# One step of delay for the cross attention's addition and an earlier first feed-forward batch in a decoder's head loop

## The reference

```python
x = x + mixer(layernorm(x))              # u @ W_b_rank @ W_b_state, butterfly of 5 levels, @ W_c_rank @ W_c_model, + D_vec * u
x = x + cross(layernorm(x), ctx, mask)   # softmax(x ctx^T / 16) ctx, no projections
x = x + ffn(layernorm(x))                # three bit-linear layers: activations rounded to 127 levels of their row's
                                         # maximum, weights to -1, 0, 1 of their mean magnitude; silu(gate) * value
...
```

## Time and profile before

| | |
|---|---|
| median of 3 runs | 1234.73 us (1233.15 to 1235.99) |
| the profiled execution's own time | 1230.95 us |
| its span | 1229.2 us |
| mean granted clock | 0.947 of full |
| DVE, ACT, POOL busy | 71%, 53%, 27% of the span |
| head, up to the first feed-forward product on DVE | 0 to 105.11 us |

### The profile page before, as it was taken

One profiled execution on the slowest core, in us unless ns is written; L12 is line 12 of the kernel. 1 busy time (PEld: TensorE's weight loads), 2 busy tenths in 40 slices (PEclk: granted clock), 3 DMA queues, 4 the chain that ended last, 5 costly groups with the idle time before them and its releaser, 6 DMA issues.

```text
span 1229.2 us, 21690 instructions
## 1 busy us (share of the span) xinstructions
PE 1058.1 (86%) x6401; PEld 729.3 (59%) x6409; DVE 874.5 (71%) x2446; ACT 654.7 (53%) x1989; POOL 333.1 (27%) x528
## 2 busy tenths in 40 slices
PE   5767887899899958899999999999998998998395
PEld 3553444666666634565667666656666665675285
DVE  4566675777887767868957778678678677765275
ACT  2757775565555615556545565565555445642262
POOL 2224231211111222313213223133132132111456
PEclk9877999999999978899999999999999999999598
...
DMA packets 38876, 49.59 MB, mean 40 GB/s; under 512 B 5110, under 2 KB 29564, under 8 KB 38528
## 3 DMA queue, kind: packets, MB, share of 16 engines
...
...
## 4 chain that ended last, share of the span: by engine, by line
PE 38%; DVE 11%; issue 6%; POOL 3%; ACT 3%; DVEq 0%; DMA 0%; ACTq 0%; POOLq 0%
PE PS L1784 35%; POOL out_dram L1376 3%; DVE arena L815 2%; DVE arena L791 1%; PE PS L2161 1%; DVE arena L827 1%; PE PS L2138 1%; ACT arena L1626 1%; POOL tokens_dram L1352 1%; DVE arena L801 1%; DVE arena L797 1%; ACT arena L1635 1%; DVE small L849 0%; DVE early L724 0%; DVE early L719 0%
## 5 line engine op out<-in xcount | busy, mean ns | idle before, releaser
L1784 PE MATMUL PS<-early,arena 128*32 128x128 f32 (+6 forms) x920 | 123.3, 362 | 51.3 <-DVE early L681 24.3
L1784 PE MATMUL PS<-EW,arena 128*128 128x128 f32 (+4 forms) x640 | 134.4, 341 | 18.0 <-DVE small L815 10.8
L1784 PE MATMUL PS<-wq,EW 128*128 128x512 f32 x256 | 128.6, 626 | 13.1 <-DVE arena L791 12.7
L1290 POOL TENSOR_SCALAR small<-small 128x4 f32<-128x4 f32 x64 | 18.8, 294 | 429.4 <-ACT mask L1619 251.6
L1784 PEld LDWEIGHTS PS<-EW,arena 128*128 128x128 f32 x640 | 99.5, 193 | 48.9 <-issue 23.5
L1784 PEld LDWEIGHTS PS<-early,arena 128*32 128x32 f32 (+4 forms) x928 | 63.2, 122 | 105.4 <-issue 39.4
L815 DVE CUSTOM_DVE_ANT_0 arena<-PS,kmask 128x128 f32<-128x128 f32 (+3 forms) x256 | 92.3, 389 | 42.4 <-PE PS L1784 34.0
L1635 ACT ACTIVATE arena<-arena,small 128x128 f32<-128x128 f32 (+3 forms) x256 | 119.5, 471 | 1.1 <-DVE small L820 0.9
L1626 ACT ACTIVATE arena<-PS 128x512 f32<-128x512 f32 x64 | 38.3, 598 | 153.1 <-PE PS L2138 153.1
L1784 PE MATMUL PS<-wo,early 128*128 128x256 f32 x512 | 113.3, 379 | 2.5 <-DVE sinT L868 1.7
L1784 PEld LDWEIGHTS PS<-wo,early 128*128 128x128 f32 x512 | 97.1, 190 | 16.4 <-DVE sinT L868 2.1
...
## 6 DMA issues: line engine op xcount, KB each, us to landing
...
```

What stands on the lines that cost most here:

```text
L1784: return pe.matmul(dst, lhs, rhs, start=first, stop=last)
```

## The change

- The cross attention's addition `read_out` of batch n moves from the end of step n + 1 to step n + 2, before that step's `cross_max`. Its PSUM bank is 6 instead of 3, the transposes' bank is 7 instead of 6, the sum of magnitudes' bank is 3 instead of 7.
- The mixer's normalising of batches 0 to 5 moves from ACT to DVE (`mix_apply`); ACT keeps 6 and 7. The batches have a semaphore of their own for it (`s_mxn`).
- The first feed-forward batch goes through the loop as a ninth batch of the mixer's kind: statistics and normalising into `aXN` in step 6, `prepare(0, 0)` and `rounded(0)` in step 7. `level_turn(0)`, `gate(0, 0)` and `value(0, 0)` stand on PE around the last batch's `cross_turn` and `cross_out` (`head_end`); the last `read_out` is in the first feed-forward half. On ACT `levels(0)`, `applied(1)` and the first silu stand inside step 8.
- One magnitude of each step moves ahead of ACT's exponents. The clippings move by about one step.
- Four of the seven small loads are issued by ACT; SP starts with batch 0. ACT runs one exponent on a single column right after, before it has other work.
- PE runs ten products of ones of 128 x 128 into bank 6 before its first real product.

```diff
+def stats_of(phase, b):
...
+    if phase == MIX:
+        return b if b < 2 else 2 * b - 1
+    return 2 * b + 2
...
 def added(phase, b):
...
+    if b < 0:
+        return 0
     if phase == MIX:
-        return max(1, 2 * b) if b >= 0 else 0
-    return min(2 * b + 3, 2 * B) if b >= 0 else 0
+        return b + 1 if b < 2 else 2 * b - 1
+    return 2 * b + 4 if b < B - 2 else B + 1 + b
...
 def piece(i):
...
         dve.wait_ge(s_x, n - B + 1)
-        if phase == FFN and type(b) is int and b == 0:
-            dve.wait_ge(s_rs, FFN * B)
+        if phase == FFN and type(b) is int and b == 1:
+            dve.wait_ge(s_rs, FFN * B + 1)
...
+        first = type(b) is int and b == 0
         dve.wait_ge(c_ap, b + 1)
-        dve.tensor_reduce(c_gx, XN[:, :, :], AX.X, ALU.max, apply_absolute_value=True).then_inc(c_q, 1)
+        dve.tensor_reduce(c_gx, aXN if first else XN[:, :, :], AX.X, ALU.max, apply_absolute_value=True).then_inc(c_q, 1)
         dve.wait_ge(c_q, 3 * b + 1)
...
         dve.wait_ge(c_q, 3 * b + 2)
-        dve.wait_ge(s_xn, FFN * B + b)
+        if not first:
+            dve.wait_ge(s_xn, FFN * B + b)
         dve.wait_ge(c_r, b + 1)
...
-        n = turn_of(phase, b)
-        if phase == MIX:
+        n = stats_of(phase, b)
+        of = b
+        if phase == CROSS:
+            dve.wait_ge(s_x, added(MIX, b))
+        elif b < B:
             dve.wait_ge(s_rows[b], 16)
         else:
-            dve.wait_ge(s_x, added(MIX, b))
+            dve.wait_ge(s_x, added(CROSS, 0))
+            of = 0
         if b > 0:
-            dve.wait_ge(s_rs, turn_of(phase, b - 1) + 1)
-        for j in range(J):
-            last = dve.bn_stats(h_st[phase][:, j, :], tokens(b, j))
+            dve.wait_ge(s_rs, stats_of(phase, b - 1) + 1)
+        if phase == MIX and b > 0:
+            dve.wait_ge(s_mxn, b)
+        for j in range(J):
+            last = dve.bn_stats(h_st[phase][:, j, :], tokens(of, j))
         last.then_inc(s_bn, 1)
...
+    def mix_apply(b):
...
+        dve.wait_ge(s_rs, stats_of(MIX, b) + 1)
+        if b > 0:
+            dve.wait_ge(s_xtp, turn_of(MIX, b - 1) + 1)
+        for j in range(J):
+            last = dve.tensor_scalar(aXN[:, j, :], tokens(b, j), h_mv[MIX][:, j, 0:1], h_rstd[MIX][:, j:j + 1],
+                                     ALU.subtract, ALU.mult)
+        last.then_inc(s_mxn, 1)
...
+    head_stats(MIX, 0)
     dve.wait_ge(s_l0, 16 * 7)
...
                                        PS[:, 4 + c, c * P:(c + 1) * P], ALU.mult, ALU.add), "mix")
+    mix_apply(1)
...
     def mix_add(b):
...
             const(dve.tensor_reduce(wsum[:, :], wpart[:, :, 0:2], AX.X, ALU.add), "wsum")
+        if n >= 2:
+            read_out(n - 2)
         if n >= 1:
             cross_max(n - 1)
-        if n + 2 < B:
+        if n + 2 <= B:
             head_stats(MIX, n + 2)
...
             dve.wait_ge(s_pp, 4)
-            const(dve.tensor_scalar(gam[:, :], PS[:, 7, 0:3], 1.0 / (D * HID), 1e-5, ALU.mult, ALU.max))
+            const(dve.tensor_scalar(gam[:, :], PS[:, 3, 0:3], 1.0 / (D * HID), 1e-5, ALU.mult, ALU.max))
             const(dve.reciprocal(rgam[:, :], gam[:, :]), "gam")
-        if n == B:
-            clip_low(5)
+        if n == B - 1:
+            prepare(0, 0)
         if n >= 1:
...
             bias_rows()
-        for i in {4: (0,), 5: (1, 2), 6: (3,), 7: (4,)}.get(n, ()):
+        for i in {5: (0, 1), 6: (2, 3), 7: (4,), 8: (5,)}.get(n, ()):
             clip_low(i)
             clip_high(i)
-        if n == B:
-            clip_high(5)
-            prepare(0, 0)
-        if n >= 1:
-            read_out(n - 1)
+        if n + 2 < ON_DVE:
+            mix_apply(n + 2)
         if n == B - 1:
-            ln_stats(FFN, 0)
-        if n == B:
             ln_stats(FFN, 1)
...
             step_size(b, j)
+            if type(b) is int and b == 0 and j == 0:
+                read_out(B - 1)
             if j == 1:
...
 def _(sp):
-    for dst, name in ((wbs, "wbs"), (wbrT, "wbrT"), (wcrT, "wcrT"), (wcm, "wcm"), (ident, "ident"), (dvec, "dvec")):
+    sp.dma_start(X[:, 0, :, :], I["x"][0].rearrange("(j p) d -> p j d", p=P)).then_inc(s_rows[0], 16)
+    sp.dma_start(factors.rearrange("p l i k -> p (l i k)"), I["factors"].partition_broadcast(NS)).then_inc(s_l0, 16)
+    for dst, name in ((ident, "ident"), (dvec, "dvec")):
         sp.dma_start(dst[:, :], I[name]).then_inc(s_l0, 16)
-    sp.dma_start(factors.rearrange("p l i k -> p (l i k)"), I["factors"].partition_broadcast(NS)).then_inc(s_l0, 16)
-    for b in range(B):
+    for b in range(1, B):
         sp.dma_start(X[:, b, :, :], I["x"][b].rearrange("(j p) d -> p j d", p=P)).then_inc(s_rows[b], 16)
...
         pool.tensor_scalar(ve[:, :], mv[:, :, 1], LN_EPS, None, ALU.add).then_inc(s_ve, 1)
-        pool.wait_ge(s_ve, n + 1 + 4 * B)
+        pool.wait_ge(s_ve, n + 1 + 2 * (2 * B + 1))
         pool.tensor_tensor(rstd[:, :], ve[:, :], halves[:, 0:J], ALU.pow).then_inc(s_rs, 1)
...
     def head_rstds(phase, b):
...
-        n = turn_of(phase, b)
+        n = stats_of(phase, b)
         k = phase
...
         if b > 0:
-            pool.wait_ge(s_xn, turn_of(phase, b - 1) + 1)
+            pool.wait_ge(*((s_mxn, b) if phase == MIX else (s_xn, 2 * b)))
         pool.tensor_tensor(h_rstd[k], h_ve[k], halves[:, 0:J], ALU.pow).then_inc(s_ve, 1)
...
         head_rstds(CROSS, b)
-        if b + 2 < B:
+        if b + 2 <= B:
             head_rstds(MIX, b + 2)
-    pool.wait_ge(s_xn, FFN * B)
-    rstds(FFN, 0)
...
     def offsets(b):
...
-    offsets(0)
     pool.wait_ge(s_abs, PIECES)
...
     scale_rows(0)
+    pool.wait_ge(s_xn, FFN * B)
     rstds(FFN, 1)
...
     out_bias(0)
+    pool.wait_ge(s_xn, FFN * B + 1)
     pool.wait_ge(s_tern, 2 * PIECES)
...
+    for dst, name in ((wbs, "wbs"), (wbrT, "wbrT"), (wcrT, "wcrT"), (wcm, "wcm")):
+        act.dma_start(dst[:, :], I[name]).then_inc(s_l0, 16)
     act.wait_ge(s_pc, 4)
+    act.activation(h_table, ones[:, 0:1], ACT.Exp)
...
     def head_apply(phase, b):
...
-        n = turn_of(phase, b)
         to = (aXN, XN)[phase]
-        act.wait_ge(s_rs, n + 1)
+        act.wait_ge(s_rs, stats_of(phase, b) + 1)
         if b > 0:
...
         for j in range(J):
-            last = act.activation(to[:, j, :], X[:, b, j, :], ACT.Identity, bias=h_off[phase][:, j:j + 1],
+            last = act.activation(to[:, j, :], X[:, b % B, j, :], ACT.Identity, bias=h_off[phase][:, j:j + 1],
                                   scale=h_rstd[phase][:, j:j + 1])
-        last.then_inc(s_xn, 1)
+        if b == B:
+            last.then_inc(c_ap, 1)
+        elif phase == MIX:
+            last.then_inc(s_mxn, 1)
+        else:
+            last.then_inc(s_xn, 2)
...
     def head_copy(phase, b):
...
     def rounded(b):
...
+        first = type(b) is int and b == 0
         act.wait_ge(c_q, 3 * b + 3)
-        after(act, s_xtp, FFN * B + b)
+        if not first:
+            act.wait_ge(s_xtp, FFN * B + b)
         act.wait_ge(c_ap, b + 1)
         for j in range(J):
-            last = act.activation(cXQ[:, j, :], XN[:, j, :], ACT.Identity, bias=magic[:, 0:1],
+            last = act.activation(cXQ[:, j, :], (aXN if first else XN)[:, j, :], ACT.Identity, bias=magic[:, 0:1],
                                   scale=c_sx[:, j:j + 1])
...
         after(act, b_o2, b)
-        act.activation(bPT[0:T, :], PS[0:T, 6, 0:S], ACT.Copy).then_inc(b_tc, 1)
+        act.activation(bPT[0:T, :], PS[0:T, 7, 0:S], ACT.Copy).then_inc(b_tc, 1)
...
     def head(n):
...
             head_copy(MIX, n + 1)
+        for i in {1: (0,), 2: (2,), 3: (4,)}.get(n, ()):
+            magnitude(i)
+        if n == B:
+            levels(0)
         if n >= 1:
...
         if n == B:
-            applied(0)
+            applied(1)
+            gated(0, 0, 0)
         if n >= 1:
...
             head_copy(CROSS, n)
-        if n + 2 < B:
+        if ON_DVE <= n + 2 <= B:
             head_apply(MIX, n + 2)
-        for i in {1: (0, 1), 2: (2, 3), 3: (4, 5)}.get(n, ()):
+        for i in {1: (1,), 2: (3,), 3: (5,)}.get(n, ()):
             magnitude(i)
...
             rounding(i)
-        if n == B:
+        if n == B - 1:
             rounded(0)
...
-    head_apply(MIX, 0)
-    head_copy(MIX, 0)
-    head_apply(MIX, 1)
-    for n in range(B + 1):
-        head(n)
...
     def evict(b, j):
...
-    levels(0)
-    applied(1)
-    gated(0, 0, 0)
+    head_copy(MIX, 0)
+    for n in range(B + 1):
+        head(n)
     over_parities(act, ffn)
...
+    pe.wait_ge(s_pc, 2)
+    for _ in range(10):
+        product(PS[:, 6, 0:P], ones[:, :], ones[:, :])
     pe.wait_ge(s_l0, 16 * 7)
...
         after(pe, b_tc, b)
-        for j in range(J):
-            last = pe.transpose(PS[0:T, 6, j * P:(j + 1) * P], bP[:, j, :], ident[:, :])
+        if b == B - 1:
+            pe.wait_ge(s_xt, FFN * B + 1)
+        for j in range(J):
+            last = pe.transpose(PS[0:T, 7, j * P:(j + 1) * P], bP[:, j, :], ident[:, :])
```

(22 more changed lines are left out.)

27 lines of the change are left out of this document (14 added, 13 removed).

## The result

| | before | after |
|---|---|---|
| median of the runs compared | 1233.95 us (1233.15 to 1235.99, 4 runs) | 1217.01 us (1214.44 to 1219.57, 4 runs) |
| profiled execution, its span | 1230.95, 1229.2 | 1219.57, 1217.6 |
| A0, A2, A5, A7, W (us) | 20.08, 35.77, 63.48, 80.39, 105.11 | 17.28, 29.32, 53.58, 67.90, 87.35 |

The changed kernel is faster by 1.3%: ratio 0.9866, 95% interval [0.9849, 0.9882], 16.9 us between the medians. 1217.0 lies inside the range of 1215 to 1235 and on the forecast's side, but the gain of the sum, 7.8 us, is less than half of the 17.8 us by which the first widened gate product (W) starts earlier in the profiled executions. Repeated on another chip the changed kernel took 1215.42 us (6 runs) beside 1230.43 (12 runs), ratio 0.9877 [0.9851, 0.9904].

A forecast was written before the change was run, and what follows sets the result against it. No engine full throughout: a step is a round trip with VectorE waiting 2.51 us, PE deciding only at 1.2 GHz. 3.7 - 3.8 + 3.7 - 0.6 + 4.8 = 7.8 us saved, 1223.15, plus half of 3.8: 1225; range 1215 to 1235.

The forecast's parts named there:

- (a): Start to VectorE's third mixer add: 3.7 us saved, that add at 32.1, set by the feed-forward weights landing at 28.3.
- none of this reaches A2: Claim that the earlier start does not reach VectorE's third mixer add, because ScalarE's first magnitude needs all feed-forward weights.
- rival 2: Feed-forward weights land no sooner, as transfer and not issue decides: third mixer add at 34.3, 1227 us, chance 0.20.
- (b): Third to fifth mixer add: 3.8 us lost, two steps of 10.7 and 7.7, the first starting at 1.2 GHz.
- (c): Fifth to sixth mixer add: 3.7 us saved, as one clipping moves on and the mixer's copy comes first.
- unavoidable gaps: VectorE's waiting from fifth to sixth mixer add, which takes 8.4 us of work to a step of 9.4.
- (d): Sixth to eighth mixer add: 0.6 us lost, 17.5 us for two steps with two clippings in each.
- (e): Eighth mixer add to first widened gate product: 4.8 us saved, first feed-forward batch prepared in the loop; 1.5 charged afterwards.
- the late second gate product: After the first widened gate product: PE's second queues behind the last cross output, losing 1.5 to 2.2 us.
- Rival 1: The clock holds from the third mixer add on, as the loop is denser: 17.4 us saved, 1215.5 us, chance 0.20.
- the stall before A2: Before the third mixer add: PE idle from about 25 to 31 us, waiting for the weights through ScalarE.
- Rivals 3 and 4: 3: gain lost at loop's end, 1232 to 1234, chance 0.12; 4: slower, clock stays at 1.2 GHz, 1239, chance 0.08.

The follow-up runs named there:

- e1: Changed kernel with all seven small loads on SP ahead of the batches and the first statistics behind the folds: 1216.95 us.
- e9: Changed kernel without the early one-element exponent, so the table load comes where ScalarE first needs it: 1216.33 us.
- e8: Changed kernel with the three feed-forward weights' transfers issued behind the attention weights: 1222.6 us.
- e3: Changed kernel with the cross attention's addition back at the end of step n + 1, for batches 0 to 6: 1217.08 us.
- e2: Changed kernel without the ten early products of ones: 1214.34 us.
- e6: Changed kernel with the last batch's cross attention again finished ahead of the first feed-forward batch's transposes and gate products: 1216.73 us.
- e7: Changed kernel with maximum, scales and rounding of the first feed-forward batch in step 8 instead of step 7: 1217.26 us.
- b1: Kernel before with four small loads on ScalarE, batch 0 first on SP and ten products of ones: 1230.76 us, ratio 1.002.

## Why the prediction was right or wrong

**(a) Start to A2: forecast +3.7, measured +6.45.** This step failed, by one number and by the statement built on it. The weights landed at 25.8 and not at 28.3: issue moved 3.1 us, the journey shrank from 17.6 to 16.0. With that, "none of this reaches A2" fell as well: e1 shows the start's gain passing through A0 (3.6) to A7 (4.2), and e9 that the table load has 1.0 us of A0. The loads that the text puts first gave 0.7 at PE's first product, not 1.3; the statistics ahead of the folds, named there without a price, gave most. The mechanism itself, a magnitude that waits for the weights, is real, and e8 shows it when the landing is late; in the changed kernel it costs 0.26 us or, in the repeat, nothing. The working from the landing to A2 was 3.8 us (28.3 to 32.1), measured 3.5 (25.81 to 29.32) and 3.2 in e8. The products of ones ended at 5.5 and, as foretold, gain nothing.

The Trainium skill ("DMA: Bandwidth & Descriptors", section "Issuing engines are not separate DMA queues") says that issuing from several engines saves no more than the time of issuing. The prediction made of that a landing at 30.5, as in rival 2, which goes further than the page, since time of issuing is saved too: here the issue came 3.1 us sooner, and the landing moved by that and 1.6 more. The 1.6 are in the journey, 17.6 us in the kernel before and 15.3 to 16.5 in every other run but e8, e1 with all loads on SP among them; why is not shown. In e8, issued 7.6 us later, at 17.42, the same transfer lands only 4.7 later, after 13.1 us, so there the issue does not decide alone.

**(b) A2 to A4: forecast -3.8, measured +1.1** (13.5 us; 12.8 in the repeat; forecast 18.4). The first step was put at 10.7 because PE would have idled for the weights. Without the wait PE was idle for only 1.2 us of the step (5.73 busy of 6.94), the clock stood at 1.00, and the step took 6.94. e8 confirms the size: with the wait, 10.06. The second step, 7.7, was taken as a chain of links laid end to end with 0.5 of gaps; the links overlap, and 6.6 is what is left. The delayed addition is the smaller part of that: e3, without it, took 7.5 and 7.0, so it is worth 0.4 to 0.6 a step.

**(c) A4 to A5: forecast +3.7 with 9.4 us, measured +2.4 with 10.74.** VectorE's work was right (8.4 forecast, 8.44 measured); "unavoidable gaps" were 2.3 us and not 1.0, in all of after, e1, e2 and e8 alike. The term was mis-sized by 1.3, 0.4 beyond its lower bound. The largest gap is the wait for the sum of magnitudes, which the earlier copy was to remove; it shrank, before and after, only from 2.10 to 1.35:

```profile
56.33 0.16 DVE L570 TENSOR_SCALAR gam<-PS 128x3 f32<-128x3 f32 x1 [2.10 <-PE PS L1784]
...
48.65 0.16 DVE L603 TENSOR_SCALAR gam<-PS 128x3 f32<-128x3 f32 x1 [1.35 <-PE PS L1823]
```

**(d) A5 to A7: forecast -0.6, measured +2.6** (14.3 us; 13.9 in the repeat). Its upper bound was +1.3 at 7.8 a step: the step from A5 took 6.45 with VectorE at 6.17 of it, so VectorE's work was 0.8 less than the 7.0 put on each step and its waiting 0.3 and not 0.8, and nothing was left there of the 1.9 us that 17.5 holds for a slower clock. Only the second step, 7.87 at 0.70, was as forecast. (By its own 22.1 the lower bound is -5.2, not -5.5.)

**(e) A7 to W: forecast +4.8, measured +5.3 to W,** less 0.6 that the late second gate product loses again in the feed-forward: +4.7. The mechanism is right, e6 and e7 show both its parts, and the order of the chain is the one laid out. That the sum is right to 0.1 is luck: two of its terms are off by 1 us each way. W was put 18.4 behind A7 at the half clock and lies 19.45 behind at 0.59 (17.41 at 0.71 in the repeat). The six gate products and six value products, put at 2.0 a set from the x17 row, account for some 0.8 of it (an estimate, from the repeat's row of six):

```profile
79.63 2.41 PE L1823 MATMUL PS<-early,arena 128*128 128x512 bf16 x6 [1.14 <-ACT arena L1485]
```

Against that, the later second silu began 2.3 after W against 1.4 before, and cost 0.6, where 1.5 was charged.

**The rivals.** Rival 1, the clock holds, is nearest to what happened (1215.5 forecast, 1217.0 measured) and got 0.20; it held from A2 to A6. Its own sum, 17.4 against the 17.8 at W, is close by luck: it has 8.6 for (e), where 5.3 came, and 4.0 for (a), where 6.45 came. The evidence against it was "the stall before A2", that is the weights' landing again: of the 10 us that the sum lacks, 2.75 are in (a), 4.9 in (b) and 3.2 in (d), less 1.3 in (c), and e8 puts back 7.1 of them by that one wait. That 1217.0 still falls within the range, 2 us inside its end, is owed to rival 1, which the range was drawn to take in, and not to the sum. Rival 2 is refuted by the landing at 25.8. Rivals 3 and 4 did not occur, though b1 shows rival 3's mechanism, a gain given back to the clock, in one execution of the old loop. Half of the 3.8 us between profiled execution and median was added back; that profiled execution of before stands under all four timed ones, and that of after is the highest of its four, so the two differ by 11.4 only, where W differs by 17.8 and the medians by 16.9.

**What is not assigned.** Taken back one at a time, the start's loads and statistics (e1), the early table load (e9), the delayed addition (e3) and the preparation in the loop (e7) move W by 4.2, 1.65, 3.4 and 3.75 us against after, 13 of the 17.8, roughly, since each is one profile. The rest was not taken apart: no run changes the PSUM banks or the place of the clippings alone.
